# A third summing bank and one more block of lag in the last layer of a graph network kernel

## The reference, cut to what matters

```python
h = relu(layernorm(x))
msg_in = concatenate([h[src], edge_features], axis=1)
messages = silu(msg_in @ mw1 + mb1)
aggregated = segment_sum(messages, dst, num_segments=N)
upd_in = concatenate([h, aggregated], axis=1)
updated = silu(upd_in @ uw1 + ub1) @ uw2 + ub2
out = x + h + updated
```

## Time and profile before

| | |
|---|---|
| median of 3 runs | 2919.78 us (2916.77 to 2933.07) |
| the profiled execution | 2890.62 us |
| its span, first to last instruction | 2888.5 us |
| mean granted clock of TensorE | 0.738 |
| last layer, from the first gather to the end | 1634.1 to 2888.5 us |

### The profile page before, as it was taken

The page is one execution under the profiler, slowest core; times in us unless marked ns, Lnnn a source line. Parts: engine busy times, 40 slices in busy tenths (PEclk is TensorE's granted clock), DMA queues, the critical chain, the costliest instruction groups (busy, mean ns, idle before and its releaser), DMA issues.

```text
span 2888.5 us, 38626 instructions
## 1 busy us (share of the span) xinstructions
PE 2074.8 (72%) x10734; PEld 1553.0 (54%) x10734; DVE 1041.5 (36%) x3131; ACT 1110.7 (38%) x2015; POOL 1830.9 (63%) x1875
## 2 busy tenths in 40 slices
PE   1588888888688888789888646566565566557566
PEld 1134444334367676467667436566465566556566
DVE  8756666566322222533443312122122122112112
ACT  4755555556456565566666311111011111111111
POOL 4556666663656663656554277777777777777775
PEclk9699999999888889798999755555555555555555
DMA  4477777676566666367666323333333333333332
GB/s 118 155 240 239 245 253 245 231 236 233 184 190 206 207 213 203 114 207 221 203 200 203 99 73 95 90 94 93 87 97 84 95 93 96 84 87 98 86 93 54
DMA packets 262383, 443.65 MB, mean 154 GB/s; under 512 B 34708, under 2 KB 211031, under 8 KB 255511
## 3 DMA queue, kind: packets, MB, share of 16 engines
q1 hardware_dynamic: 196744, 259.07, 29.4%
q0 software_dynamic: 58224, 119.35, 14.9%
q10 hardware_dynamic: 7200, 62.72, 5.5%
HBM read 360.58 MB, written 80.42 MB: 153 GB/s over the span
## 4 chain that ended last, share of the span: by engine, by line
another core or an unknown queue 28%; PE 27%; DVE 6%; issue 5%; DVEq 3%; ACT 1%; POOL 0%; DMA 0%; POOLq 0%; ACTq 0%
PE bank L1057 12%; PE bank L1007 7%; PE bank L1087 4%; DVEq L1467 1%; DVE onehot L1461 1%; DVE msg L1555 1%; DVE acc L1471 1%; ACT unit L517 1%; DVE unit L517 1%; PE bank L1102 1%; DVEq L1488 0%; PE bank L1173 0%; PE bank L1103 0%; POOL gath L776 0%
## 5 line engine op out<-in xcount | busy, mean ns | idle before, releaser
L776 POOL DMA_INDIRECT gath<-table,src_sb x1644 | 1596.9, 971 | 811.2 <-issue 496.4
L1007 PE MATMUL bank<-onehot,msg 128*128 128x31 f32 x1662 | 367.8, 375 | 430.3 <-DVE acc L1471 241.8
L1057 PE MATMUL bank<-unit,halves 128*128 128x500 f32 x1960 | 579.0, 440 | 108.0 <-ACT unit L517 53.0
L1007 PEld LDWEIGHTS bank<-onehot,msg 128*128 128x128 f32 x1662 | 365.4, 316 | 472.7 <-issue 446.4
L1471 DVE TENSOR_TENSOR acc<-acc,bank 128x31 f32 (+1 forms) x548 | 105.8, 193 | 1349.1 <-remote 943.0
L517 ACT CAST unit<-region 128x500 fp32r<-128x500 f16 x840 | 458.6, 606 | 248.5 <-PE bank L1057 196.1
L945 ACT ACTIVATE msg<-msg 128x384 f32<-128x384 f32 x277 | 144.4, 522 | 1022.7 <-DVE msg L1555 612.0
L1057 PEld LDWEIGHTS bank<-unit,halves 128*128 128x128 f32 x1960 | 385.5, 210 | 225.5 <-ACT unit L517 77.4
L862 ACT CAST shared<-bank 128x490 f32 x600 | 373.6, 623 | 252.4 <-PE bank L1029 150.3
L1087 PE MATMUL bank<-mw,region 128*128 128x128 f32 x1662 | 428.8, 425 | 6.5 <-issue 4.5
L1087 PEld LDWEIGHTS bank<-mw,region 128*128 128x128 f32 x1662 | 369.3, 316 | 21.2 <-issue 21.1
(11 more groups left out here) (149 smaller groups left out, 1377.2 us busy)
## 6 DMA issues: line engine op xcount, KB each, us to landing
region<-counts SPq DMA_DIRECT2D x196, 875.0 KB
counts<-shared ACTq DMA_DIRECT2D x50, 1225.0 KB
region<-in_edge_T SPq DMA_DIRECT2D x138, 384.0 KB
gath<-table,src_sb POOLq DMA_INDIRECT x1644
table<-shared SPq DMA_DIRECT2D x36, 256.0 KB, 2.3
table<-parts SPq DMA_DIRECT2D x12, 384.0 KB, 2.6
acc<-in_x SPq DMA_DIRECT2D x12, 256.0 KB, 5.3
shared<-in_x SPq DMA_DIRECT2D x12, 256.0 KB
```

The source lines that it names most:

```text
L776: pool.indirect_dma_start(out=(gath if l > 0 else gath_parts)[:, BT * place + j, :], out_offset=None, in_=table[l], in_offset=bass.Indirec ...
L1007: mm = nc.tensor.matmul(summed_in(l, n)[:, 0:W], of, onehot[:, n % HOTS, j, :], start=(j == 0), stop=(j == BT - 1))
L1057: mm = nc.tensor.matmul(sum_bank(ordinal), halves[:, hi, a, :], units[h][:, :], start=(hi == 0 and a == 0), stop=(hi == NTILE - 1 and a == 1))
```

## The change

The last layer gets three summing banks in place of two, banks 0, 1 and 2. `sum_block(3, n)` now waits for the addition of block n - 3. DVE adds three blocks back in place of two. The one-hots of this layer lie in an array of their own with twelve places, and are made four blocks ahead: four before the loop, then `hot(n + 4)` behind `add(n - 3)`. As bank 2 is now used for sums, the updates of chunks and their rows (all but the last chunk's) go to bank 7, and the first update waits until ACT has copied all 13 node shares out of that bank.

```diff
-SUM_BANKS = [2, 5, 2, 2]
+SUM_BANKS = [2, 5, 2, 3]
...
-ADD_LAG = 2
+ADD_LAG, HOT_LEAD, LAST_HOTS = 3, 4, 12
...
+        last_onehot = over("last_onehot", [P, LAST_HOTS, BT, W], F32, parts_at + 4 * REST)
...
         def update_bank(c):
-            return bank[2 if c < NCH - 1 else 3]
+            return bank[7 if c < NCH - 1 else 3]
 
         def result_bank(c):
-            return 2 if c < NCH - 1 else 4
+            return 7 if c < NCH - 1 else 4
...
-                        mm = nc.tensor.matmul(summed_in(l, n)[:, 0:W], of, onehot[:, n % HOTS, j, :], start=(j == 0), stop=(j == BT - 1))
+                        mm = nc.tensor.matmul(summed_in(l, n)[:, 0:W], of, (last_onehot[:, n % LAST_HOTS, j, :] if l == 3 else onehot[:, n % HOTS, j, :]), start=(j == 0), stop=(j == BT - 1))
...
                 after(pe, st[4]["rows_ready"], c if c < NCH - 1 else 0)
+                if c == 0:
+                    pe.wait_ge(st[4]["z_ready"], NCH)
...
-                    after(dve, block_summed, BLOCKS_BEFORE[l] + n - HOTS + 1)
+                    after(dve, block_summed, BLOCKS_BEFORE[l] + n - (LAST_HOTS if l == 3 else HOTS) + 1)
                     b = rel[:, bass.ds(FIRST[l] + n, 1), :].rearrange("p o t -> p t o").to_broadcast([P, BT, W])
-                    nc.vector.tensor_tensor(onehot[:, n % HOTS], iota_w, b, ALU.is_equal).then_inc(onehot_ready, 1)
+                    to = last_onehot[:, n % LAST_HOTS] if l == 3 else onehot[:, n % HOTS]
+                    nc.vector.tensor_tensor(to, iota_w, b, ALU.is_equal).then_inc(onehot_ready, 1)
...
                     left_edges(3)
+                    for n in range(HOT_LEAD):
+                        hot(n)
                     for n in range(NB + RESULT_AT):
-                        if n < NB:
-                            hot(n)
                         if n < NB:
                             add_features(n)
                         if ADD_LAG <= n < NB + ADD_LAG:
                             add(n - ADD_LAG)
+                        if n + HOT_LEAD < NB:
+                            hot(n + HOT_LEAD)
```

## The result

| | before | after |
|---|---|---|
| median of the runs on the same chip | 2918.77 us (2912.91 to 2933.07, 6 runs) | 2900.16 us (2890.69 to 2906.82, 6 runs) |
| ratio, 95% interval | | 0.9932 [0.991, 0.9953] |
| profiled execution, and its span | 2890.62, 2888.5 us | 2902.36, 2900.3 us |

The change makes the kernel faster by 18.6 us, 0.7%. The two profiled executions say the opposite, and must not be set against each other: that of before was shorter than every timed run of its kernel beside it (2912.91 at the least), and it carries the rows on which the prediction rests. Why it was short stays open. It isn't known on which chip it was taken, and chips differ by more than the change: the medians of this same kernel are 2918.77 to 2934.31 us in four of the comparisons here and 2892.55 (2883.22 to 2897.20) in the one on another chip (short_rests_after).

The account below looks back on a forecast made before the run. POOL was taken to bound the last layer, with 75 us of waits on DVE to win. Fewer stalls gave 9 us, all other parts 0: 2919.8 - 9 = 2911 us, own range 2905 to 2914, wide range 2862 to 2926.

Parts of the forecast that it names:

- The bound and its ceiling: Last layer: POOL sets the pace, 4.18 us a block; its 75.2 us of waits on `msg` are all to win.
- Late by a fixed time, or told at a limited rate: Slow stretch of the last layer: PE's completions are told in order at a limited rate, one block in 8.04 us.
- rival A: Completions have a fixed delay, so three banks give 5.4 us a block; 50 to 75 us go, 2855 us; chance 0.17.
- up to 20: Expected profile sign: an addition releases up to 20 us behind its sum's end, since three are under way.
- The third bank and lag 3: Last layer's loop: one more block of slack means fewer POOL stalls, 9 us less, between 6 and 12.
- bit over half: Share of cycles above the lower bound (6 us) in which the extra block was counted, giving 9 us.
- the 26 update places: 13 `add_share` and 13 `result` on DVE: waiting there empties the slack whatever the lag, so the lower half is favoured.
- The one-hots, bank 7 and the tail: Earlier one-hots, updates in bank 7 and the end behind the last gather: each 0 us, the tail at most 0.3.
- The idle time ahead of the additions: DVE in the last layer: 895.1 us, to become not much smaller since the slow 8 us a block stays.
- B: The change does nothing, as messages stay tied to edge products: 0 to 3 us, 2918 us; chance 0.18.
- C: Slower: POOL's gathers wait for one more product pair at 13 chunk updates, 33 us, 2953 us; chance 0.12.
- D: TensorE is granted 1.00 clock in more stretches behind stalls, nearly all 75 us go, 2848 us; chance 0.03.

Follow-up runs that it names:

- short_rests_after: The changed kernel with POOL's clearings half as long (512 columns) and ahead of every block: 2871.59 us beside 2892.55 for the kernel before, ratio 0.9928.
- same_as_before: The kernel before, unchanged, timed and profiled again as a null comparison: 2924.88 us, ratio 1.0.
- one_hots_only: The kernel before with only the one-hots made four blocks ahead in twelve places, still two banks and a lag of two: 2925.18 us, ratio 0.9997.
- banks_and_lag_only: The kernel before with third sum bank, additions three blocks back and updates in bank 7, but the old one-hots: 2908.29 us, ratio 0.9945.
- same_as_after: The changed kernel, unchanged, timed and profiled again: 2910.71 us, ratio 0.9961 to the kernel before.
- one_update_after: The changed kernel with edge products sending no completion of their own from the fourth block on: 2922.04 us, ratio 0.996 to the kernel before (2934.31).
- one_edge_product_after: The changed kernel with one edge product of three a block, the others left out: 2884.44 us, ratio 0.9879 to the kernel before.

## Why the forecast was right and wrong

**The bound and its ceiling** hold. POOL at 8.32 us for two blocks (2371.82 to 2380.14) and its waits on `msg` are what the loop can win; on average the layer became shorter by what these waits lost. But the ceiling was read too low: 75.2 us come from an execution shorter than any run timed beside it, and the two-bank ones of same_as_before and one_hots_only have 92 to 94. The prediction had seen the 29.2 us between the median and the profiled execution, "which I can't place". Between the spans of the two profiled executions of the kernel before are 33.7 us (2922.2 - 2888.5): 19.6 of them lie ahead of the layer (first gather at 1653.64, not 1634.09), 14.2 in it, where the waits are 18.9 longer.

**Late by a fixed time, or told at a limited rate**: against rival A the reading of the earlier trace rows was right. Slow stretches go at 8.06 us with three banks, the release of a sum went from 11.3 to 22.2 us ("up to 20"), and most of the stalls stayed (28 on average). As a rate of PE's side it was wrong, or at least too simple: fewer instructions (7.11 us) and half as many completions (8.37) leave it about where it was, and only POOL's pauses moved it far. The Trainium skill (Perfetto Trace Analysis, Tensor Engine Instruction) has the semaphore come behind the shown end of a matmul; the trace agrees, with 22.2 us.

**The third bank and lag 3** is the term that was mis-sized. It said 9 us, between 6 and 12; the traces show 12 and the timed comparisons 11 to 20 (the interval of the result, 0.991 to 0.9953, begins at 13.7 us). Its way of counting holds: fewer stalls of the same length, 33.5 of 2.9 us to 28 of 3.0. A stall came every 277 / 33.5 = 8.3 blocks and now comes every 277 / 28 = 9.9, so the extra block is worth 1.6 blocks of POOL's, between the 1 and the 2.1 of the prediction and near its "bit over half". What was off is the number that it started from, 26 stalls, one every 10.65 blocks, out of the short execution. The same working from 33.5 stalls of 2.9 us gives, as an estimate, 29.9 to 26.7 stalls and 10 to 20 us less. That the traces' 12 us equals the top of the recorded range is chance, then. All this leans on two and three executions, and their counts scatter (31 and 36; 29, 29 and 26).

The part that it took off for the 26 update places, "which empties the slack whatever the lag", can't be judged by itself. The idle time there grew, from 94.4 us in same_as_before (51.1 and 43.3) to 169.0, but ahead of messages and additions it fell by more, from 929.8 (25.0 and 904.8) to 831.3: 23.9 us less over the four groups. The waits traded places.

**The one-hots, bank 7 and the tail** had been put at nothing: 0.9997 for the first; no separate run for bank 7, whose cost is within the gain of banks_and_lag_only. From the last gather's start to the end it is 22.05 us after (2878.25 to 2900.3) and 22.5 before (2865.99 to 2888.5): the tail is 0.5 us shorter, where 0.3 had been allowed.

**The idle time ahead of the additions** was to be "not much smaller". It halved, by the lag alone, and meant nothing: with the message's it went down by a tenth only, as just shown. The prediction should have asked where DVE, with one more block between them, meets a late completion first.

**The rivals.** A falls by the pace; B by the gain; C has its sign (L1546 at 76.8 us from 45.8) but not its price, because these waits came out of others; D doesn't show: the granted clock of the slow and of the dense stretch after is 0.50 in both, and from 1660 to 2900 us its mean is 0.52, where it was 0.54 before. Windows of the changed kernel (busy us of PE, PEld, DVE, ACT, POOL, then the clock, DMA share, GB/s):

```profile
2366.00:2391.00 25.00, 11.54 (x38) 9.41 (x37) 2.85 (x11) 1.57 (x3) 19.93 (x22) 0.50 0.29 79
2391.00:2400.00 9.00, 6.64 (x30) 6.76 (x31) 4.16 (x15) 2.36 (x5) 4.80 (x6) 0.50 0.44 121
```

So the forecast had the right direction and, but for the cause of the rate, the right mechanism. It lay 11 us above the median, which is below its own range of 2905 to 2914 us and inside the wide one of 2862 to 2926, and it called "no change that can be told" the likeliest where a gain just above it came out; three other comparisons (same_as_after, banks_and_lag_only, one_update_after) put it at 0.4 to 0.55%, the result's own at 0.7%.

## What to carry on

A profiled execution is one draw, and perhaps of another chip: before its waits are used as a ceiling, set its time against the range of the runs, and where it lies below, expect more stalls than it shows. Count stalls by their length: a count of waits also holds distances that are the usual ones. When slack is added ahead of an engine that stalls often, look at the sum over all places of the waiting engine, since a longer lag only moves its idle time from one line to another. And a pause on the bound engine may be what feeds the others: leaving POOL's clearings out freed some 133 us and cost 0.7%.

## What had not been expected of the hardware

While POOL issues indirect gathers every 1.25 us (0.95 and 0.30 idle), PE's completions reach the other engines long after the modelled end: 22.2 us in the cycle shown, and 24.7 us at the most in that execution (the sum that ends at 2579.80, added at 2604.54 after 7.25 us of idle time). In the slow stretches shown they come at one block in 7.1 to 8.4 us, whether two or three blocks are under way, with 16 or 24 instructions of PE for a block, and with one or two completions told for it. Without POOL's pauses the distance grew to 10.7 and 12.0 us. PE's own products are stretched too, once three banks let it run ahead (145.7 us of idle time within them, from 5.4), at a mean clock of 0.52; with one edge product in three the same three banks leave 2.8 us (one_edge_product_after). What is shared between POOL's gathers and PE's completions none of these runs shows; that stays open, as does how long a pause must be.
